# Six windowed attention layers: reciprocal lengths seeded by exp(-ln/2) on ScalarE, and masks as two products over separate row halves

## The chip, the core and the metric

One core of a Trainium2 chip. The metric is the device time of one execution in microseconds (us). Engines: TensorE (PE; its weight loads are shown apart as PEld), VectorE (DVE), ScalarE (ACT), GpSimd (POOL) and the DMA queue of SyncE (SP). Each runs its own instructions in order and waits for the others through semaphores.

## The reference, cut to what matters

`x` is 8 sequences of 512 rows of 128 numbers. It is normalized, sent through a causal attention with relative positions, and, beside that, through six layers of windowed attention and feed-forward. The change touches the windowed attention only:

```python
def l2norm(t):
    return t / jnp.maximum(jnp.linalg.norm(t, axis=-1, keepdims=True), 1e-12)
# 16 heads of 64, windows of 32 queries, 64 keys each (own window and the one before)
q = l2norm(q) * qs;  k = l2norm(k) * ksc
q = q * cos * scale + rotate_half(q) * sin * scale      # k likewise, with 1 / scale
mask = (it < jb) | (it > jb + w) | (jb == -1)
sim = jnp.einsum('bhwie,bhwje->bhwij', bq, bk2) * QK_SCALE
sim = jnp.where(mask, -jnp.finfo(sim.dtype).max, sim)
out = einsum(softmax(sim), bv2) @ Wo
for i in range(6):
    x = attn_layer(shift_tokens(x), ...) + x
    x = ffn_layer(shift_tokens(x), ...) + x
```

## The kernel before, in words

`relative_attention` does the first attention (to about 560 us). `windowed_layers` then runs six layers, five in a hardware loop and the last one behind it. In each layer the 32 tiles of 128 rows (8 sequences by 4) go through a pipeline of slots: in the slot of tile T the engines project tile T (age 0), turn and score tile T-1 (age 1) and finish the softmax, the mixing and the output of tile T-2 (age 2). The order within a slot is written out by hand for every engine in a function called `slot`, and what one engine needs of another it waits for by counted semaphores. The two slots at the end of a layer (CLOSING and LAST) have no new tile and take in the first steps of the feed-forward part, which `feed` goes on with. `opening` projects the first tile of the next layer inside `feed`, so the first slot of a layer is that of tile 1.

TensorE in a full slot, in order: projection of v, k, k, q (each three products of 512 columns, L1250 to L1252), turning the first half of the weights (transposes, L1264), projection of q, turning the other weights, mixing (64 small products, L1288), turning q, mixing, projection of v, turning k, the mixed values, k again, then the two mask products (L1404), scores of four head pairs (L1274), output (L1410), scores of the other four. A mask product writes one PSUM bank (2 or 3, 128 rows by 512 columns) as identity times mask with start=True; the scores of even heads are then added into bank 2, those of odd heads into bank 3, by products with 64 contracting rows and 32 outputs each, head parity being the row half.

The lengths of T: ScalarE squares q and k (L1562), VectorE sums the squares by head (`square_sum`, L1747), and `square_root` bounds the 128x32 sums below (L1755), seeds the reciprocal root by a shift and a subtraction on number bits (L115, L117), halves the sums (L118) and does one Newton step (L121, L123, L125). GpSimd, which has meanwhile added the two parts of the rotated k and q (L1176), takes the result, does two more steps (`rsqrt_refine`, L139 to L145, eight instructions) and scales q and k by it (L1181). TensorE turns q and k in the next slot once they are scaled. On odd tiles GpSimd also makes the low part of the next inputs (L1057), after ScalarE has made the high part (`split_half`). VectorE's next work after the lengths is the output's addition (L1826) and then the maxima of the scores (L1782), the differences (L1788), from which ScalarE makes the weights by Exp (`weigh`, L1587).

ScalarE's functions come in table sets. Gelu (L1664) and Exp are in different ones, so a layer loads two.

Of the kernel before, what the change touches and what calls it, by code (L numbers as in the profile page):

```python
# [27 lines left out]
P = 128  # L28
B, N, D = 8, 512, 128
TPS = N // P  # L30
H = 16
# [3 lines left out]
W = 32  # L35
# [18 lines left out]
C_NEAR = C_FART + P  # L54
# [6 lines left out]
def constants():  # L61
# [21 lines left out]
    first = (np.arange(P)[:, None] < W) & (k2 < W)  # L83
    c[:, C_MQ0:C_MQ0 + 2 * W] = np.where(first, MASKED, shut)
    far = np.where(np.arange(P)[None, :] >= np.arange(P)[:, None], MASKED, 0.0)
    c[:, C_FAR:C_FAR + P] = far
    c[:, C_FART:C_FART + P] = far.T
# [785 lines left out]
def windowed_layers(nc, Wqkv, qs, ks, Wout, ln_g, ln_b, W1, b1, W2, b2, state, total, rank, out):  # L873
# [8 lines left out]
    with ExitStack() as ctx:  # L882
# [24 lines left out]
        half_ss, rn_tmp = sb("half_ss", [P, 2 * H]), sb("rn_tmp", [P, 2 * H])  # L907
# [26 lines left out]
        id_bf, mask_bf, mean_w = rank["id_bf"], rank["mask_bf"], rank["mean_w"]  # L934
# [3 lines left out]
        FIRST_STEPS, MORE_STEPS = 1, 2  # L938
        RN_FIRST, RN_MORE = 1 + 3 + 3 * FIRST_STEPS, 4 * MORE_STEPS
# [25 lines left out]
        rn_chain, rn_more = sem("rn_chain"), sem("rn_more")  # L965
# [183 lines left out]
        def _(pool):  # L1149
# [18 lines left out]
            def rope_and_scale(lay, s, t):  # L1168
# [16 lines left out]
                pool.wait_ge(rn_chain, RN_FIRST * (T + 1))  # L1185
# [61 lines left out]
        def _(pe):  # L1247
# [45 lines left out]
            def slot(lay, s, t, ages):  # L1293
# [106 lines left out]
                if score:  # L1400
                    turn_k(1)
                    pe.wait_ge(on_made, at(T, 2, 2, 2))
                    for par in range(2):
                        pe.matmul(PS[:, 2 + par, :], id_bf[:], bc(mask_q[tile1], 1, PAIRS),  # L1404
                                  start=True, stop=False, skip_group_check=True)
                    score_half(0)
# [127 lines left out]
        def _(act):  # L1534
# [18 lines left out]

            def high_part(lay, i):
                act.wait_ge(raw_in[i], 16 * lay + 16)
                last_projected(act, lay)
                copy(w_hi[:, third(i)], w_raw[:, third(i)]).then_inc(hi_made, 1)
# [22 lines left out]
            def slot(lay, s, t, ages):  # L1580
# [67 lines left out]
                if 0 in ages:  # L1648
                    new = next_half(s, t)
# [17 lines left out]
            def feed(lay, follows):  # L1667
# [15 lines left out]
                if follows:  # L1683
                    split_half(lay + 1, 0, 1)
# [6 lines left out]
            copy(credit[:, 47:48], zeros[:, 0, 0:1]).then_inc(gel_made, 2)  # L1691
            high_part(0, THIRDS[0])
# [3 lines left out]
            for n in range(len(OPENING)):  # L1696
                opening(0, n)
            split_half(0, 0, 1)
# [6 lines left out]
        def _(dve):  # L1705
# [44 lines left out]
            def square_root(T):  # L1750
# [4 lines left out]
                dve.tensor_scalar(ss[:], ss[:], 1e-24, None, ALU.max).then_inc(rn_chain, 1)  # L1755
                dve.wait_ge(rn_chain, RN_FIRST * T + 1)
                rsqrt_steps(dve, rn_chain, RN_FIRST * T + 1, rn[:], ss[:], half_ss[:], rn_tmp[:], FIRST_STEPS)
# [12 lines left out]
            def lengths(T):  # L1770
                square_sum(T, 0, sqq_made)
                square_sum(T, 1, sqk_made)
                square_root(T)
# [177 lines left out]
```

## Time and profile before

| | us |
|---|---|
| median of 3 runs | 3954.44 (3954.09 to 3967.59) |
| the profiled execution | 3959.98 |
| its span, first to last instruction | 3958.2 |
| mean granted clock of TensorE | 0.982 of full speed |

Busy shares of the span by the profile's page: PE 94%, PEld 72%, DVE 83%, ACT 55%, POOL 66%. To read the rows: times are us from the span's start, "xN" counts instructions, and what stands in square brackets is the idle time of the engine just ahead of the row and who ended it. A matmul's start is recorded and its end is modelled, so overlapping products show in the distances of their starts, not in their busy time. "issue" is idle time for which the profile shows nothing to wait for.

### The profile page before, as it was taken

To read this page: it belongs to the slowest core of one execution; us is meant where nothing else is said; L and a number is where in the kernel's file an instruction comes from. 1 tells how busy PE (TensorE), PEld (TensorE's weight loads), DVE (VectorE), ACT (ScalarE), POOL (GpSimd) and SP (SyncE) were. 2 spreads that over 40 slices of the span, in tenths; PEclk is the share of its full clock that TensorE was granted. 3 is DMA by queue.
4 is the path that set the end of the run, shared out by engine and by line. 5 is a ranking of instruction groups with operands and counts; after the bars stand their busy time and mean duration, and the time that the engine had idled before them with its cause. 6 is when DMAs were issued, how large, how long until landed. Compare 5 with 4: busy or idle time off the path is not lost.

```text
span 3958.2 us, 165481 instructions
## 1 busy us (share of the span) xinstructions
PE 3716.9 (94%) x67712; PEld 2864.8 (72%) x67712; DVE 3286.9 (83%) x6981; ACT 2178.6 (55%) x3886; POOL 2598.7 (66%) x3029
## 2 busy tenths in 40 slices
PE   6999979999999999999999999999999999999998
PEld 3555547878767787677787677787677776777776
DVE  7666659999789899788998798997889897888886
ACT  3555545666546666456665465665466564565552
POOL 4555538887457777368787287874577773687770
PEclk8999989999999999999999999999999999999999
DMA  1000012222212222122222122222122221222220
GB/s 43 4 6 4 6 34 66 57 56 59 58 34 58 60 60 58 35 53 56 60 60 52 33 65 60 56 57 56 35 57 60 60 56 37 53 55 59 60 52 22
DMA packets 136325, 189.11 MB, mean 48 GB/s; under 512 B 38006, under 2 KB 58484, under 8 KB 135412
## 3 DMA queue, kind: packets, MB, share of 16 engines
q1 hardware_dynamic: 135540, 178.17, 17.6%
q8 instruction: 551, 9.03, 1.0%
q14 instruction: 234, 1.92, 0.2%
HBM read 22.61 MB, written 2.10 MB: 6 GB/s over the span
## 4 chain that ended last, share of the span: by engine, by line
POOL 39%; PE 22%; issue 20%; DVE 2%; POOLq 2%; ACT 0%; DMA 0%; SPq 0%; DVEq 0%; ACTq 0%
POOL t L1176 18%; POOL t L1181 8%; PE PS L1264 3%; PE PS L1250 3%; POOL xl L1057 3%; PE PS L1469 2%; PE PS L1252 2%; PE PS L1251 2%; POOL rn L145 2%; PE PS L1410 2%; POOL rn_tmp L141 2%; POOL rn_tmp L143 2%; POOL rn_tmp L139 2%; PE PS L1288 2%; PE PS L1274 1%
## 5 line engine op out<-in xcount | busy, mean ns | idle before, releaser
L1176 POOL TENSOR_TENSOR t<-t 128x1024 f32<-128x1024 f32 x384 | 908.3, 2373 | 263.3 <-DVE t L1742 263.3
L1535 ACT ACTIVATE va<-PS 128x512 f32<-128x512 f32 x384 | 230.1, 599 | 956.3 <-PE PS L1252 956.3
L1181 POOL TENSOR_TENSOR t<-t,rn 128x1024 f32<-128x1024 f32 x384 | 724.1, 1907 | 28.4 <-POOL rn L145 25.9
L1740 DVE TENSOR_TENSOR t<-PS,rope 128x512 f32<-128x512 f32 x768 | 521.7, 679 | 23.6 <-ACT sq L1562 18.1
L1250 PE MATMUL PS<-w_hi,xh 128*128 128x512 f32 x1152 | 514.8, 447 | 25.7 <-DVE xl L1057 10.1
L1562 ACT ACTIVATE sq<-PS 128x512 f32<-128x512 f32 x768 | 455.7, 594 | 38.3 <-PE PS L1252 22.3
L1252 PE MATMUL PS<-w_lo,xh 128*128 128x512 f32 x1152 | 460.8, 400 | 0.0
L1251 PE MATMUL PS<-w_hi,xl 128*128 128x512 f32 x1152 | 458.9, 398 | 0.0
L1264 PE MATMUL PS<-constants,t 128*128 128x128 f32 x3072 | 444.7, 278 | 9.5 <-POOL t L1181 7.6
L1747 DVE TENSOR_REDUCE ss<-sq 128x16 f32<-128x1024 f32 x384 | 448.0, 1207 | 0.0
L1264 PEld LDWEIGHTS PS<-constants,t 128*128 128x128 f32 x3072 | 352.8, 142 | 58.2 <-POOL t L1181 9.9
L1410 PE MATMUL PS<-oT,w_out 128*128 128x128 f32 x3072 | 393.3, 281 | 0.0
L1288 PE MATMUL PS<-vs,shared 64*32 64x65 f32 x18432 | 337.2, 225 | 45.3 <-issue 45.3
L1410 PEld LDWEIGHTS PS<-oT,w_out 128*128 128x128 f32 x3072 | 357.8, 191 | 17.7
L1274 PEld LDWEIGHTS PS<-kT,qT 64*32 64x32 f32 x24576 | 273.9, 105 | 127.3 <-issue 103.3
L1274 PE MATMUL PS<-kT,qT 64*32 64x64 f32 x24576 | 342.7, 225 | 15.0 <-POOL kT L1210 7.8
L1288 PE MATMUL PS<-va,shared 64*32 64x65 f32 x6144 | 338.9, 225 | 14.6 <-issue 14.6
L1288 PEld LDWEIGHTS PS<-vs,shared 64*32 64x32 f32 x18432 | 265.0, 105 | 111.0 <-issue 110.8
L1741 DVE TENSOR_TENSOR t<-PS,rope 128x256 f32<-128x256 f32 x768 | 316.3, 412 | 0.0
L1742 DVE TENSOR_TENSOR t<-PS,rope 128x256 f32<-128x256 f32 x768 | 315.8, 411 | 0.0
L1782 DVE TENSOR_REDUCE m<-PS 128x16 f32<-128x1024 f32 x192 | 234.9, 1224 | 87.4 <-PE PS L1274 85.2
L1250 PEld LDWEIGHTS PS<-w_hi,xh 128*128 128x128 f32 x1152 | 218.3, 190 | 95.7 <-issue 30.0
(172 smaller groups left out, 8112.8 us busy)
## 6 DMA issues: line engine op xcount, KB each, us to landing
vs<-va SPq DMA_DIRECT2D x768, 130.0 KB
vs<-va SPq DMA_DIRECT2D x768, 65.0 KB
t<-in_L_ffn_Wqkv SPq DMA_DIRECT2D x18, 512.0 KB, 4.4
w_out<-in_L_ffn_Wo SPq DMA_DIRECT2D x6, 512.0 KB, 3.9
a_normed<-in_L_attn_x SPq DMA_DIRECT2D x8, 256.0 KB, 6.4
a_xo<-in_L_attn_x SPq DMA_DIRECT2D x8, 256.0 KB, 2.9
out<-total SPq DMA_DIRECT2D x8, 256.0 KB, 3.5
w_raw<-in_L_ffn_W SPq DMA_DIRECT2D x6, 341.0 KB
```

What stands on the lines that cost most here:

```text
L1176: pool.tensor_tensor(mine[:, i, :], mine[:, i, :], t2[:, i, :], ALU.add).then_inc(done, 1)
L1181: pool.tensor_tensor(h, h, bc(rn[:, H * i:H * (i + 1)], 2, HB), ALU.mult).then_inc(done, 1)
L1250: pe.matmul(out, hi, w_hi, start=True, stop=False)
L1251: pe.matmul(out, lo, w_hi, start=False, stop=False)
L1252: return pe.matmul(out, hi, w_lo, start=False, stop=True)
L1264: last = pe.transpose(PS[:, bank, P * j:P * (j + 1)], source(j), ident)
L1274: last = pe.matmul(PS[W * w:W * (w + 1), 2 + par, 2 * W * pair:2 * W * (pair + 1)], qT[rows, pair, W * w:W * (w + 1)], kT[rows, t % 2, pai ...
L1288: last = pe.matmul(PS[W * w:W * (w + 1), (0, 2)[c] + par, HB1 * (pair % 4):HB1 * (pair % 4 + 1)], pT[rows, pair, W * w:W * (w + 1)], v, st ...
L1410: last = pe.matmul(PS[:, y_at, 0:P], w_out[:, pair, :], oT[:, pair, :], start=(pair == 0), stop=(pair == PAIRS - 1))
L1562: act.activation(sq[:, i, 512 * c:512 * (c + 1)], PS[:, bank, :], ACT.Square).then_inc(done, 1)
L1740: dve.tensor_tensor(o1, src, bc(rope[:, 2 * i, t, :], 1, 8), ALU.mult)
L1747: dve.tensor_reduce(ss[:, H * i:H * (i + 1)], sq[:, i, :].rearrange("p (h d) -> p h d", h=H), X, ALU.add).then_inc(ss_made, 1)
```

## The change

The bound and the halving become one VectorE instruction with two operations. The seed is made on ScalarE as exp(-ln(-2 * half)/2), two instructions of 128x32, in the same table set, which is loaded ahead of it (and of the layer's later Exp). VectorE's six further instructions go. GpSimd's two Newton steps stay. ScalarE's `seed(T)` stands behind the second k copy of the slot and ahead of `split_half`; in `feed` it stands behind the last piece of the opening.

The mask products contract over 64 rows each, rows 0 to 63 for bank 2 and rows 64 to 127 for bank 3, with a new 128x128 constant that selects for each query its row of the mask within a half. The constants grow by 128 columns. In the diff below, the pieces behind `seed` are those of ScalarE's `slot`, its `feed`, its start ahead of the first layer, and GpSimd's `rope_and_scale`.

```diff
+C_SEL = C_FART + P
-    first = (np.arange(P)[:, None] < W) & (k2 < W)
+    first = (np.arange(P)[:, None] % (2 * W) < W) & (k2 < W)
+    row, query = np.arange(P)[:, None] % (2 * W), np.arange(P)[None, :]
+    c[:, C_SEL:C_SEL + P] = np.where(query < W, query == row, query % W + W == row)
...
                     for par in range(2):
-                        pe.matmul(PS[:, 2 + par, :], id_bf[:], bc(mask_q[tile1], 1, PAIRS),
+                        rows = slice(HB * par, HB * (par + 1))
+                        pe.matmul(PS[:, 2 + par, :], sel_bf[rows, :], bc(mask_q[tile1][rows, :], 1, PAIRS),
                                   start=True, stop=False, skip_group_check=True)
...
-            def square_root(T):
+            def half_squares(T):
                 dve.wait_ge(ss_made, at(T, 0, 2, 2))
                 dve.wait_ge(kn_made, at(T, 1, 1, 1))
-                dve.tensor_scalar(ss[:], ss[:], 1e-24, None, ALU.max).then_inc(rn_chain, 1)
-                dve.wait_ge(rn_chain, RN_FIRST * T + 1)
-                rsqrt_steps(dve, rn_chain, RN_FIRST * T + 1, rn[:], ss[:], half_ss[:], rn_tmp[:], FIRST_STEPS)
+                dve.tensor_scalar(half_ss[:], ss[:], 1e-24, -0.5, ALU.max, ALU.mult).then_inc(half_made, 1)
...
+            def seed(T):
+                act.wait_ge(half_made, T + 1)
+                act.activation(ln_ss[:], half_ss[:], ACT.Ln, scale=-2.0).then_inc(ln_made, 1)
+                act.wait_ge(ln_made, T + 1)
+                act.activation(rn[:], ln_ss[:], ACT.Exp, scale=-0.5).then_inc(seed_made, 1)
...
                 if 0 in ages:
+                    seed(T)
                     new = next_half(s, t)
...
                 if follows:
+                    act.preload_act_table_set("natural_log_exp_and_others")
+                    seed(number(lay + 1, 0, 0))
                     split_half(lay + 1, 0, 1)
...
+            act.preload_act_table_set("natural_log_exp_and_others")
...
+            seed(0)
             split_half(0, 0, 1)
...
-                pool.wait_ge(rn_chain, RN_FIRST * (T + 1))
+                pool.wait_ge(seed_made, T + 1)
```

## Rows read from the trace of the kernel before

**Rows 1.** The page's engine line, and the stretch of 30 slots of layer three.
```profile
PE 3716.9 (94%) x67712; PEld 2864.8 (72%) x67712; DVE 3286.9 (83%) x6981; ACT 2178.6 (55%) x3886; POOL 2598.7 (66%) x3029
...
1716.20:2155.50 439.30, 423.79 (x9707) 346.44 (x9705) 399.89 (x870) 267.78 (x514) 348.33 (x422) 1.00 0.24 59
```

**Rows 2.** The chain that ended last, shares of the span by engine.
```profile
POOL 39%; PE 22%; issue 20%; DVE 2%; POOLq 2%; ACT 0%; DMA 0%; SPq 0%; DVEq 0%; ACTq 0%
```

**Rows 3.** Timeline of TensorE around one slot: start, duration, line, tiles, count.
```profile
1199.83 0.60 PE L1264 MATMUL PS<-constants,t 128*128 128x128 f32 x4
1200.27 0.59 PE L1404 MATMUL PS<-mask_bf,id_bf 128*128 128x512 bf16 x2
1200.79 0.86 PE L1274 MATMUL PS<-kT,qT 64*32 64x64 f32 x64
...
1204.35 0.50 PE L1250 MATMUL PS<-w_hi,xh 128*128 128x512 f32 x1
...
1218.83 0.49 PE L1250 MATMUL PS<-w_hi,xh 128*128 128x512 f32 x1
```

**Rows 4.** Waits of TensorE over the span: total, times, longest.
```profile
PE PS L1288 <- issue: 59.9, 76, 1.5
```

**Rows 5.** Timeline of TensorE in that slot: four transposes, then the small mixing products.
```profile
1208.62 0.60 PE L1264 MATMUL PS<-constants,shared 128*128 128x128 f32 x4
1209.15 0.24 PE L1288 MATMUL PS<-vs,shared 64*32 64x65 f32 x1
```

**Rows 6.** Groups by form over the span: the mask products (busy, mean ns, idle before).
```profile
L1404 PE MATMUL PS<-mask_bf,id_bf 128*128 128x512 bf16 x384 | 115.2, 382 | 0.0
```

**Rows 7.** Timelines around one slot's lengths, and ScalarE's 128x128 Exp by form.
```profile
1202.36 0.20 DVE L1755 TENSOR_SCALAR ss<-ss 128x32 f32<-128x32 f32 x1
1203.56 0.19 DVE L125 SCALAR_TENSOR_TENSOR rn<-rn_tmp,rn 128x32 f32<-128x32 f32 x1
1203.83 0.24 POOL L139 TENSOR_TENSOR rn_tmp<-rn 128x32 f32<-128x32 f32 x1 [1.31 <-DVE rn L125]
1201.21 0.85 ACT L1535 ACTIVATE xh<-state 64x256 fp32r<-64x256 f32 x2
1205.36 0.60 ACT L1535 ACTIVATE va<-PS 128x512 f32<-128x512 f32 x1 [3.29 <-PE PS L1252]
L695 ACT ACTIVATE a_p<-a_d 128x128 f32<-128x128 f32 x8 | 2.5, 312 | 0.0
```

**Rows 8.** Timelines of four engines in a layer's first slot: layer six, then layer one.
```profile
3400.68 0.50 PE L1250 MATMUL PS<-w_hi,xh 128*128 128x512 f32 x1
3398.66 2.29 DVE L115 TENSOR_SCALAR rn<-ss 128x32 int32<-128x32 int32 x1
3403.98 1.22 DVE L1782 TENSOR_REDUCE m<-PS 128x16 f32<-128x1024 f32 x1
3398.55 4.72 POOL L1176 TENSOR_TENSOR t<-t 128x1024 f32<-128x1024 f32 x2
3404.15 0.24 POOL L139 TENSOR_TENSOR rn_tmp<-rn 128x32 f32<-128x32 f32 x1 [0.88 <-DVE rn L125]
3406.77 3.77 POOL L1181 TENSOR_TENSOR t<-t,rn 128x1024 f32<-128x1024 f32 x2
3406.01 1.28 ACT L1587 ACT_TABLE_LOAD   x1 [3.02 <-DVE shared L1788]
3411.74 1.06 PE L1264 MATMUL PS<-constants,t 128*128 128x128 f32 x6
...
606.73 1.09 PE L1264 MATMUL PS<-constants,shared 128*128 128x128 f32 x4 [2.56 <-ACT shared L1587]
```

**Rows 9.** Timelines of GpSimd and VectorE in the closing slot of layer two.
```profile
1597.57 0.24 POOL L139 TENSOR_TENSOR rn_tmp<-rn 128x32 f32<-128x32 f32 x1 [1.31 <-DVE rn L125]
...
1604.35 2.04 POOL L1201 TENSOR_TENSOR t<-t 128x512 f32<-128x512 f32 x2
1607.53 0.17 DVE L1715 TENSOR_SCALAR f_var<-PS 128x8 f32<-128x8 f32 x1 [3.12 <-PE PS L1440]
```

More of the change, by code:

```diff
@@ L53 @@
 C_FART = C_FAR + P
-C_NEAR = C_FART + P
+C_SEL = C_FART + P
+C_NEAR = C_SEL + P
 C_PART = C_NEAR + H
@@ L906, in windowed_layers @@
         halves3 = sb("halves3", [P, 2 * H])
-        half_ss, rn_tmp = sb("half_ss", [P, 2 * H]), sb("rn_tmp", [P, 2 * H])
+        half_ss, rn_tmp, ln_ss = sb("half_ss", [P, 2 * H]), sb("rn_tmp", [P, 2 * H]), sb("ln_ss", [P, 2 * H])
         qT = sb("qT", [P, PAIRS, P])
@@ L933, in windowed_layers @@
         ident = rank["const"][:, C_ID:C_ID + P]
-        id_bf, mask_bf, mean_w = rank["id_bf"], rank["mask_bf"], rank["mean_w"]
+        mask_bf, mean_w = rank["mask_bf"], rank["mean_w"]
+        sel_bf = mask_bf[:, C_SEL - C_MQ:C_SEL - C_MQ + P]
         mask_q = {t: mask_bf[:, 2 * W * (t == 0):2 * W * (t == 0) + 2 * W] for t in range(TPS)}
         RN_OPS = RSQRT_OPS + 1
-        FIRST_STEPS, MORE_STEPS = 1, 2
-        RN_FIRST, RN_MORE = 1 + 3 + 3 * FIRST_STEPS, 4 * MORE_STEPS
+        MORE_STEPS = 2
+        RN_MORE = 4 * MORE_STEPS
         CREDIT = 4
@@ L964, in windowed_layers @@
         ss_made = sem("ss_made")
-        rn_chain, rn_more = sem("rn_chain"), sem("rn_more")
+        half_made, ln_made, seed_made, rn_more = sem("half_made"), sem("ln_made"), sem("seed_made"), sem("rn_more")
         addq_made, addk_made = sem("addq_made"), sem("addk_made")
@@ L1772, in lengths @@
                 square_sum(T, 1, sqk_made)
-                square_root(T)
+                half_squares(T)
             def slot(lay, s, t, ages):
```

## The prediction

> **What bounds the kernel now.** I read four views, from the coarse to the fine. The busy shares come first: in 30 slots of layer three, 439.3 us or 14.6 us a slot, TensorE is busy for 423.8, VectorE for 399.9, GpSimd for 348.3 and ScalarE for 267.8 [rows 1]. The chain that ended last puts 39% on GpSimd and 22% on TensorE [rows 2], so the second question is which of the two a slot waits for. The chain follows GpSimd from one add to the next, but the adds wait for VectorE, which waits for the scores, which are TensorE's. So I went to TensorE's timeline. One slot runs from 1204.35 to 1218.83, 14.48 us [rows 3], and its products start at distances that their columns set: four transposes take 0.44 (1199.83 to 1200.27), the masks 0.52 (to 1200.79). What remains idle in most slots is inside the small products, put down to "issue": 59.9 us at L1288 in 76 waits [rows 4], of which the change touches nothing. GpSimd, 1.3 us of idle time in its lengths included [rows 7], is a follower with some slack. So in a full slot only what TensorE itself does counts, and the lengths count only where TensorE does wait: in the first slot of a layer and in the first closing slot.
>
> **The change part by part. The seed.** Removed from VectorE is the stretch from the end of L1755 (1202.36 + 0.20) to the end of L125 (1203.56 + 0.19), 1.19 us; the one instruction left costs what L1755 costs, 0.20 [rows 7]. GpSimd started its steps at 1203.83, 1.27 behind L1755. In its place come two ScalarE instructions of 128x32. The trace has none of that size; a 128x128 one takes 0.31 [rows 7], which bounds each from above, and I take 0.25. With three hand-overs of some 0.08 each (L125's end at 1203.75 to 1203.83) that is 0.75, so GpSimd begins about 0.5 us earlier; the bounds are 0.4 (0.31 each and hand-overs of 0.09) and 0.8 (ScalarE at the 0.2 that small instructions of VectorE take, hand-overs hidden in part).
>
> In a full slot this is worth nothing. It is covered by TensorE's own 14.5 us; if that cover were gone, GpSimd would be the bound, and the 0.5 would count in full.
>
> What is queued behind the new wait on ScalarE: `split_half` (0.85) and then the next slot's copy of v, which frees bank 7 for the q product. The high part was made at 1201.21, now about 1203.3 to 1204.1, and the v copy starts at 1205.36 after 3.29 us of waiting for TensorE [rows 7]. So 1.2 us are left and this costs nothing. At the opening of the first layer and ahead of the last, where no loop turn lies between, the margin is smaller and up to 1 us may be lost once each; I take 1 in all. The low part on GpSimd comes two scalings later and is not late.
>
> **First slots.** Here the small VectorE instructions stand beside GpSimd's long add (4.72 us from 3398.55), and two of them are held until one of its halves ends: L115 took 2.29 instead of 0.2, and the next one as long [rows 8]. The maxima, ready to start at about 3400.8, when the scores have ended (TensorE's next product starts at 3400.68), start at 3403.98. The change takes these instructions away, so the maxima come 3.2 us earlier, and in the last layer the Exp table's load of 1.28, which stood behind the differences, has gone ahead too. TensorE would reach the turning of q 4.5 us earlier, at 3407.2. But GpSimd is late next: its steps began at 3404.15 and can begin no earlier than the add's end, 3403.27; the first of the two scalings, 1.9 of the 3.77 from 3406.77, then ends at 3407.8 instead of 3408.7. So q is turned at about 3407.9 instead of 3411.74: 3.8 us. The same working on the first layer, where TensorE waited 2.56 for the weights [rows 8], gives 2.3, and on the four between 0.6, 2.7, 0 and 0.6. Six first slots: 10 us. Should the remaining instruction be held once (up to 2.3), the maxima still start near the scores' end; the low bound is 5. The high bound is 14: behind layer one's wait the four transposes take 1.09 instead of 0.60 [rows 5, 8], as at half the clock, and shorter waits may save some of that.
>
> **Closing slots.** GpSimd's 1.31 wait for the seed [rows 9] is followed, without a gap, by its steps, the scaling and the squares of the feed-forward norm (from 1604.35); VectorE waits 3.12 us for the sums of these squares, and TensorE in turn for VectorE's root. Here the 0.5 counts: 6 x 0.5 = 3 us.
>
> The table loads stay two a layer, at 1.28 each [rows 8]. The one that moves into `feed` stands where ScalarE has to wait for VectorE's sums anyway, and the one added ahead of the first layer is followed by the wait for the rope's scales. Both cost nothing.
>
> The Trainium skill (ScalarE: Activation LUTs, What ACT_TABLE_LOAD costs) gives 1.28 us and 1.38 of drain, 2.66 in all. The trace agrees with the first figure [rows 8]; of the second no row here tells.
>
> **The masks.** Now two products of 512 columns start 0.21 apart (0.59 for both less the 0.38 of one [rows 3, 6]), and the scores start 0.31 behind the second, of which 0.21 are its columns and 0.10 the change to 64 rows. The same 0.09 to 0.10 stand between transposes and mixing: 0.53 for four transposes instead of 0.44 [rows 3, 5]. From the last transpose to the first score it is 0.11 + 0.21 + 0.31 = 0.63 us. After: the change to 64 rows comes ahead of the masks (0.11 + 0.09 = 0.20), the two start together if the halves work side by side (0.01), and the scores, which have other output columns, start 0.31 behind: 0.52, a gain of 0.11. The weights of 128 columns can't be loaded ahead over such a change; no row shows their cost in this form, and I take 0.03 to 0.05 for it from the 0.10 that a mask's load leaves under its predecessor now. So 0.07 a slot. In the six first slots TensorE waits behind the mask anyway, so 186 x 0.07 = 13 us. Part of it is lost where TensorE next stands in an "issue" wait, which depends on when its instructions were fetched and not on when it arrives; a quarter gives 10 us. Bounds: -0.15 a slot (side by side fails, the load shows), -28 us; and +0.21 (the second product free, the first change no dearer than the one behind it, which goes), +39 us.
>
> The Trainium skill (TensorE: Matmul & The Clock Gate, Measured speedup vs the span model) has four products over 32 rows each at 512 columns run 3.07 times as fast as in a row, which speaks for the overlap. It also says (TensorEngine Tiling (Array Packing), Key Properties) that changing the tiling mode drains TensorE; that is the 0.10 of rows 3 and 5, and it speaks against this edit, since a second such change may be bought for one product.
>
> The constants grow by a sixteenth or so and load once, under 0.5 us.
>
> **The sum.** 10 + 3 + 10 - 1 = 22 us. From the profiled execution's 3960.0 that makes 3938; this execution lies 5.5 above the median of the runs shown, 3954.4, so the forecast in runs is 3932.
>
> **The rivals.** (A) The forecast, 3932: 0.37. (B) The halves don't work side by side: the masks take 0.21 + 0.09 more than hoped, so 0.09 to 0.15 a slot is lost, 17 to 28 us, against 12 gained elsewhere: 3960 to 3970, slower than before. For it: no row shows two products over 64 rows that fill all 128 outputs, and the small products are spaced by their weight loads, so their overlap by row halves isn't proven. It decides where two masks take more than 0.32 from start to the scores plus 0.10. 0.18. (C) The masks gain nothing, because two changes and a bare weight load eat the 0.2, or because the "issue" waits do: 12 us, 3942. Nothing in the rows speaks against it, 0.25. (D) The change between the two 64-row forms is free and the gain per slot is 0.2: 186 x 0.2 = 37, plus 12: 3905. The change from 128 to 32 outputs alone would have to cost nothing. 0.15. (E) It doesn't do what it says: the table sets alternate in every slot, each load of 1.28 standing ahead of the weights, for which TensorE is waiting or about to. 186 x 1.28 is 238 us; with half of it covered it is 119, so 4060 or above. The set named has both functions. 0.02. The rest, 0.03, is a start of the first layer or an alignment of TensorE's fetches that comes out worse.
>
> The gain of the seed in first and closing slots, 12 us, is in A to D alike. The range takes in A and C whole, B up to 3964 and D down to 3906: 3906 to 3964.
>
> Chances, where 0.5% (20 us, about what a measurement of this kernel can tell from no change) divides: faster, under 3934.7, is D, most of A and the top of C, 0.46; slower, over 3974, is E, the end of B and half of the rest, 0.08; within 0.5%, 0.46. The likeliest case, A, has a range of its own, 3925 to 3938.
>
> **What would show it.** Right, if GpSimd's L139 starts about 0.75 behind the new VectorE instruction; if the maxima of the first slots follow the scores' end at once; if the waits of ScalarE's va copy stay above a microsecond; if the second mask starts within 0.05 of the first, with the scores 0.3 behind it. Wrong, if a row of the va copy is released by anything but TensorE, if a table load stands in a full slot, or if the two masks start 0.2 apart. The prediction as a whole falls if full slots change in length by more than 0.2 us either way, since 186 of them outweigh all that the seed does.

## The result, and the profile after

| | before | after |
|---|---|---|
| median of 7 runs each | 3965.22 (3954.09 to 3969.12) | 3937.53 (3927.25 to 3938.96) |
| ratio | | 0.9933, interval 0.9916 to 0.9950 |
| profiled execution, its span | 3959.98, 3958.2 | 3928.65, 3926.6 |

The change saves 27.7 us. The forecast of 3932 was the level of the kernel before, 3954.4, less a gain of 22. The three runs before on which it stood were low: the seven give 3965, and in four later comparisons the median of the same kernel lay between 3962 and 3972. So the level was 11 us too low and the gain 6 us too small, and the two errors partly cancel in the forecast. A single execution says little below 10 us: the runs of either kernel spread over 12 to 15.

The page of the kernel after: its engine line, then the stretch of the same 30 slots of layer three, from first mask to first mask (columns as in [rows 1]).

```profile
PE 3690.6 (94%) x67712; PEld 2844.7 (72%) x67712; DVE 3058.0 (78%) x5829; ACT 2270.7 (58%) x4270; POOL 2597.4 (66%) x3029
...
1710.26:2149.40 439.14, 424.51 (x9852) 347.21 (x9852) 364.05 (x693) 283.68 (x576) 351.24 (x428) 1.00 0.24 61
```

Thirty slots with VectorE 36 us less busy, and with GpSimd's steps started some 0.67 us earlier (below), take the same 439 us as before [rows 1]. So the lengths don't set this stretch. It doesn't show the 0.11 a slot that the masks save either, 3 us in thirty slots; the experiments below say where that goes. The chain that ended last now follows TensorE, where before it followed GpSimd for 39% [rows 2]:

```profile
PE 76%; issue 4%; DVE 2%; POOL 2%; ACT 0%; DMA 0%; POOLq 0%; SPq 0%; DVEq 0%; ACTq 0%
```

That line looks like a change of regime, and it isn't one: full slots are within 0.1 us of what they were. That two engines are nearly as long as each other here, so that a shift of 0.7 us decides which of them the chain is led along, is my reading and not tested.

TensorE's timeline at the masks of one slot, which answers [rows 3]:

```profile
1210.13 0.60 PE L1270 MATMUL PS<-constants,t 128*128 128x128 f32 x4
1210.66 0.39 PE L1411 MATMUL PS<-mask_bf 64*128 64x512 bf16 x2
1210.98 0.86 PE L1280 MATMUL PS<-kT,qT 64*32 64x64 f32 x64
```

Two products of 512 columns now take 0.39 together; before they took 0.59. From the transposes' row to the scores' it is 0.85 instead of 0.96 (1199.83 to 1200.79). By the starts of single products, medians of 192 slots that hardly vary: last transpose to first mask 0.109 before and 0.205 after, mask to mask 0.215 and 0.003, mask to score 0.309 and 0.316. In sum 0.633 and 0.524.

The waits of TensorE at the mixing products, as in [rows 4]: 4.5 us more than before.

```profile
PE PS L1294 <- issue: 64.4, 87, 1.4
```

The seed, in the closing slot of layer two (VectorE, then GpSimd): GpSimd begins 0.80 behind the start of VectorE's instruction, where it was 1.47 (1202.36 to 1203.83, [rows 7]); from that instruction's end it is 0.60 instead of 1.27. Its wait is 0.64 instead of 1.31. VectorE's wait for the sums of the squares is 2.76 instead of 3.12 [rows 9]. By form, over the span, the two new instructions take 229 ns each.

```profile
1590.18 0.20 DVE L1775 TENSOR_SCALAR half_ss<-ss 128x32 f32<-128x32 f32 x1
1590.98 0.24 POOL L144 TENSOR_TENSOR rn_tmp<-rn 128x32 f32<-128x32 f32 x1 [0.64 <-ACT rn L1567]
...
1601.15 0.17 DVE L1735 TENSOR_SCALAR f_var<-PS 128x8 f32<-128x8 f32 x1 [2.76 <-PE PS L1447]
...
L1565 ACT ACTIVATE ln_ss<-half_ss 128x32 f32<-128x32 f32 x192 | 44.0, 229 | 239.9 <-DVE half_ss L1775 239.9
L1567 ACT ACTIVATE rn<-ln_ss 128x32 f32<-128x32 f32 x192 | 44.0, 229 | 6.1
```

The first slot of layer six, which answers [rows 8] (VectorE, GpSimd, ScalarE, TensorE):

```profile
3374.73 1.96 DVE L1775 TENSOR_SCALAR half_ss<-ss 128x32 f32<-128x32 f32 x1
3376.61 1.21 DVE L1800 TENSOR_REDUCE m<-PS 128x16 f32<-128x1024 f32 x1
3374.29 4.73 POOL L1182 TENSOR_TENSOR t<-t 128x1024 f32<-128x1024 f32 x2
3378.97 0.24 POOL L144 TENSOR_TENSOR rn_tmp<-rn 128x32 f32<-128x32 f32 x1
3376.72 0.23 ACT L1565 ACTIVATE ln_ss<-half_ss 128x32 f32<-128x32 f32 x1 [2.84 <-DVE half_ss L1775]
3383.56 1.09 PE L1270 MATMUL PS<-constants,t 128*128 128x128 f32 x8 [1.58 <-POOL t L1187]
```

One VectorE instruction is still held (1.96 instead of 0.20) until the first of GpSimd's two additions ends; before there were two in a row. The maxima stand at VectorE's first free moment, GpSimd goes on with no wait, and TensorE, as forecast, now waits 1.58 for GpSimd's scaled q. It does so in all twelve first slots of two traces of the change: q is turned 0.05 to 0.06 behind the end of GpSimd's first scaling.

Where the 31.6 us between the two profiled spans lie (a slot is measured from the start of its first mask product to the next slot's):

| | before | after | gain |
|---|---|---|---|
| ahead of the first mask | 598.4 | 597.4 | 1.0 |
| 6 first slots | 105.0 | 88.0 | 17.0 |
| 174 full slots | 2533.3 | 2521.8 | 11.5 |
| 6 closing slots | 122.6 | 121.9 | 0.7 |
| 5 times ending and feed | 503.9 | 501.4 | 2.5 |
| behind the last mask | 95.0 | 96.2 | -1.2 |

### The profile page after: what moved, and what is told of

It reads as the page before. It is cut to its first block, busy times and chain, and to the rows that moved or that the text cites. A ratio compares the mean times of both kernels' runs of the same rounds, so it can differ in the third digit from the quotient of the medians.

```text
span 3926.6 us, 163773 instructions
## 1 busy us (share of the span) xinstructions
PE 3690.6 (94%) x67712; PEld 2844.7 (72%) x67712; DVE 3058.0 (78%) x5829; ACT 2270.7 (58%) x4270; POOL 2597.4 (66%) x3029
## 4 chain that ended last, share of the span: by engine, by line
PE 76%; issue 4%; DVE 2%; POOL 2%; ACT 0%; DMA 0%; POOLq 0%; SPq 0%; DVEq 0%; ACTq 0%
PE PS L1270 18%; PE PS L1417 10%; PE PS L1256 10%; PE PS L1294 8%; PE PS L1280 8%; PE PS L1258 8%; PE PS L1257 8%; PE PS L1476 2%; PE PS L1411 2%; PE PS L1454 1%; PE PS L1447 1%; POOL t L1182 1%; PE PS L1442 1%; POOL t L1187 0%; DVE m L1800 0%
## 5 line engine op out<-in xcount | busy, mean ns | idle before, releaser
L1182 POOL TENSOR_TENSOR t<-t 128x1024 f32<-128x1024 f32 x384 | 908.0, 2370 | 363.9 <-DVE t L1762 362.6
L1542 ACT ACTIVATE va<-PS 128x512 f32<-128x512 f32 x384 | 229.8, 599 | 614.4 <-PE PS L1258 611.6
L1270 PE MATMUL PS<-constants,t 128*128 128x128 f32 x3072 | 443.8, 277 | 19.8 <-POOL t L1187 12.8
L1256 PEld LDWEIGHTS PS<-w_hi,xh 128*128 128x128 f32 x1152 | 217.4, 189 | 92.5 <-issue 24.7
```

The lines of the kernel that those rows point to most:

```text
L1182: pool.tensor_tensor(mine[:, i, :], mine[:, i, :], t2[:, i, :], ALU.add).then_inc(done, 1)
L1256: pe.matmul(out, hi, w_hi, start=True, stop=False)
L1270: last = pe.transpose(PS[:, bank, P * j:P * (j + 1)], source(j), ident)
```

## The experiments

All ratios are against the kernel before in the same comparison. "Second halves" are the mean lengths of the second half of the mixing and of the scores in full slots, where the waits ended by issue show: undisturbed, each takes 0.79. The profile counts 64 instructions in such a half where the code has 32 products. The last three columns are from single traces; two traces of one kernel differ by 0.015 and 0.025 in the mean full slot.

| kernel | ratio (interval) | mean full slot | 6 first slots | second halves |
|---|---|---|---|---|
| before, two traces | 1 | 14.559, 14.544 | 105.0, 107.6 | 1.21, 0.91; 1.21, 0.89 |
| the change, two traces | 0.9933 (0.9916 to 0.9950), 0.9920 (0.9898 to 0.9942) | 14.493, 14.518 | 88.0, 86.0 | 1.23, 0.92; 1.25, 0.93 |
| seed only | 0.9934 (0.9910 to 0.9958) | 14.487 | 90.7 | 1.17, 0.89 |
| masks only | 0.9981 (0.9963 to 0.9998) | 14.455 | 107.2 | 1.19, 0.92 |
| masks on one row half | 0.9977 (0.9960 to 0.9995) | 14.574 | 87.5 | 1.12, 0.84 |
| one step on GpSimd | 0.9908 (0.9881 to 0.9935) | 14.471 | 80.9 | 1.23, 0.91 |
| before, all steps on GpSimd | 1.0033 (1.0018 to 1.0048) | 14.625 | 109.0 | 1.13, 0.90 |
| scores together | 1.0158 (1.0138 to 1.0178) | 14.965 | 88.0 | see there |
| the same, one step | 1.0133 (1.0111 to 1.0156) | 15.033 | | |
| values between mixings | 0.9906 (0.9888 to 0.9925) | 14.441 | 89.4 | 0.86, 0.83 |
| the same, one step | 0.9884 (0.9864 to 0.9904) | 14.467 | 79.0 | 0.87, 0.84 |
| halving on GpSimd | 0.9941 (0.9920 to 0.9961) | 14.538 | 94.6 | |

**The two parts apart.** The change with the masks as before:

```diff
-                        rows = slice(HB * par, HB * (par + 1))
-                        pe.matmul(PS[:, 2 + par, :], sel_bf[rows, :], bc(mask_q[tile1][rows, :], 1, PAIRS),
+                        pe.matmul(PS[:, 2 + par, :], id_bf[:], bc(mask_q[tile1], 1, PAIRS),
```

> The lengths' part of the change alone, with the masks as they were. My theory: it pays only where TensorE waits, in the six first slots (17 us in the profile of the changed kernel, 105.0 to 88.0) and little elsewhere, so the ratio to the kernel before is 0.9950 to 0.9965 (14 to 20 us). Full slots keep their length of 14.56 us on average within 0.03. Rival, that the lengths' chain through GpSimd, which the chain of waits of before put ahead of TensorE, sets the full slots too: these get shorter by 0.06 us or more, and this kernel is as fast as the whole change, 0.993.

Measured: 3938.22, ratio 0.9934, as fast as the whole change. And the kernel before with the masks of the change (the same lines the other way round, and the constants with them):

> The masks' part alone, with the lengths as they were. My theory: from the last transpose to the first score it takes 0.52 instead of 0.63 us, and of these 0.11 a slot some 0.06 arrive at the slot's end, 186 x 0.06 = 11 us, so a ratio of 0.997 (0.9955 to 0.9985), and the two parts add up to the whole. Rival, that the masks' gain is given back in full in the waits for instructions: ratio 0.9990 to 1.001, and the full slots stay at 14.56.

Measured: 3955.80, ratio 0.9981. The savings alone are 0.0066 and 0.0019, 0.0085 in sum; together they measured 0.0067 and 0.0080. So they add within the intervals, and the seed has about three quarters of it. The size I gave the seed is refuted, and both numbers of the rival came true (0.993, and full slots shorter by 0.065). Its mechanism, GpSimd's chain in full slots, is what the two experiments on GpSimd's steps speak against. The trace of the seed alone shows 90.7 us of first slots against 105.0 and 107.6.

In full slots the single traces don't add up: 0.065 with the seed alone, 0.097 with the masks alone (14.455), and 0.046 with both. The profiled execution of the masks alone was 9 us below the median of its runs, which is 0.05 a slot. So one trace doesn't tell how 0.05 of a full slot is shared out; the medians are what the shares above rest on.

**Side by side, or only 64 rows?** Both products on rows 0 to 63:

```diff
-                        rows = slice(HB * par, HB * (par + 1))
+                        rows = slice(0, HB)
```

> The whole change, but both mask products contract over rows 0 to 63, which hold the same masks, so they can't run side by side and the result is the same. My theory: the second mask starts 0.21 behind the first again, the first slot score 0.73 behind the last transpose instead of 0.52, and a full slot is longer than in the changed kernel by 0.13 to 0.21 us, 25 to 40 us in all: 3962 to 3977 against 3937, ratio to the kernel before 0.999 to 1.003. Rival, that the overlap doesn't matter because TensorE has slack at this place: within 5 us of the changed kernel.

Measured: 3956.03, ratio 0.9977, 18 us behind the change where I had 25 to 40, and full slots 0.06 to 0.08 longer where I had 0.13 to 0.21. TensorE's timeline in that kernel:

```profile
1210.14 0.60 PE L1270 MATMUL PS<-constants,t 128*128 128x128 f32 x4
1210.68 0.60 PE L1411 MATMUL PS<-mask_bf 64*128 64x512 bf16 x2
1211.21 0.97 PE L1280 MATMUL PS<-kT,qT 64*32 64x64 f32 x64
...
PE PS L1294 <- issue: 49.0, 67, 1.2
```

Mask to mask is 0.226 and transpose to mask 0.205, as in the change. So the 0.003 comes from the separate row halves, and the price of going to 64 rows, 0.096, is paid in both. The waits row shows what becomes of such time: masks and first scores take 0.29 us a slot more than in the change (0.21 and 0.08), and mixing waits 15 us less for issue; the two second halves are 0.11 and 0.08 shorter. Of 0.29, 0.06 to 0.08 arrives at the slot's length.

**One step less on GpSimd.** `MORE_STEPS = 1` in the change, so that GpSimd does four operations of 0.33 instead of eight:

> The whole change with one Newton step on GpSimd instead of two, four instructions less a tile, 1.3 us of GpSimd's chain. My theory: full slots don't get shorter, since GpSimd has slack there; the first slots do, where TensorE waits about 1.6 us for the scaled q (2.25 to 2.44 at the mixing products instead of 0.79), by 1.3 each, and the closing slots by up to 1 each: 8 to 12 us under the changed kernel, ratio to the kernel before 0.990 to 0.9915. Rival, that GpSimd is still a part of the full slots' length: 0.2 us or more a slot, 35 us and more, ratio 0.984 or less.

Measured: 3926.02, ratio 0.9908. The first slots fall from 88.0 to 80.9: 7 us, or six times 1.2, nearly the 1.3 of the step. It is GpSimd's chain that first slots wait for after the change. With the step gone, q is turned behind the scaling at once in two of the six, and 1.2 to 1.5 later in the other four. Full slots keep their length within 0.05. GpSimd's wait for VectorE ahead of the additions takes up the rest (the page's row, which reads 363.9 in the change):

```profile
L1182 POOL TENSOR_TENSOR t<-t 128x1024 f32<-128x1024 f32 x384 | 909.2, 2369 | 595.1 <-DVE t L1762 595.1
```

**One step more on GpSimd.** The kernel before, with VectorE's step moved there (`FIRST_STEPS, MORE_STEPS = 0, 3`):

> The kernel before with its one refining step on VectorE moved to GpSimd (0 steps there, 3 on GpSimd), masks and seed bits as before. VectorE loses three operations of 0.19 us, GpSimd gains four of 0.33 us, 1.3 us a slot, against 263.3 us / 192 = 1.37 us a slot in which GpSimd waited for VectorE. My theory (full slots are not set by the chain of the lengths, so it may move by a microsecond either way): full slots within 0.1 us of 14.56, the six first slots 0 to 8 us longer in sum, ratio 0.998 to 1.004. Rival (GpSimd is at its edge in full slots, and the part of the seed's gain that full slots show comes from an earlier start of GpSimd): full slots longer by 0.3 to 1.3 us, ratio 1.013 to 1.06.

Measured: 3984.87, ratio 1.0033. Full slots are 0.07 to 0.08 longer, 13 us in sum; first slots 1 to 4 us longer, closing slots 132.2 instead of 122.6 and 124.0. Each lies where the theory had it except the closing slots, which I had not priced: there GpSimd's steps are followed by the squares of the norm without a gap, and the six lost 1.2 to 2.4 each, 1.6 in the mean. The products that spread the root begin 0.6 later in four of them and 1.5 in two (VectorE's own chain is shorter by its three operations); the rest is TensorE's clock, which stands at half for 45 us in the six slots instead of 24 and 30. The edit adds one wait besides, VectorE for the end of its own chain. Full slots have room for a GpSimd 1.3 us busier, but not quite for nothing.

**Scores in one piece.** The second half of the scores directly behind the first, ahead of the output; VectorE's addition of the output behind the next maxima:

```diff
                     score_half(0)
+                    score_half(1).then_inc(s_mm, 1)
                 if mix:
                     pe.wait_ge(oT_made, at(T, 2, 2, 2))
...
                     last.then_inc(y_mm, 1)
-                if score:
-                    score_half(1).then_inc(s_mm, 1)
```

> The change, and the second half of the scores directly behind the first, ahead of the output products, so that TensorE goes from 64-row to 128-row products and back once a slot and not twice; VectorE adds the output of a slot to the state behind the maxima of the next. Theory: each passage costs what the first mask product showed, 0.095 us, so two fewer are 0.19 us a slot, 35 us in 186 slots, a quarter of it lost to waits for instructions: ratio 0.985 to 0.989 against the kernel before, and 0.992 to 0.996 of the change. Rival: 128 small products in a row want instructions faster than they come, and the gain goes into waits ended by issue, or the maxima are later and GpSimd with them: ratio 0.992 to 0.998.

Measured: 4034.73, ratio 1.0158. Slower by 62 us, and both my cases had it faster. Timeline of TensorE in one slot, with ScalarE's second copy of the turned k, and two rows of TensorE's waits:

```profile
1827.05 0.39 PE L1411 MATMUL PS<-mask_bf 64*128 64x512 bf16 x2
1827.37 1.57 PE L1280 MATMUL PS<-kT,qT 64*32 64x64 f32 x106
1827.39 0.63 ACT L1541 ACTIVATE kT<-PS 128x512 f32<-128x512 f32 x1
1828.24 0.53 PEld L1280 LDWEIGHTS PS<-kT,qT 64*32 64x32 f32 x43 [0.18 <-issue]
1830.28 0.42 PE L1280 MATMUL PS<-kT,qT 64*32 64x64 f32 x22 [1.34 <-issue]
...
PE PS L1280 <- issue: 94.4, 63, 2.2
PE PS L1294 <- issue: 26.5, 40, 2.1
```

Two things happen here. After 106 score products TensorE stands still for 1.34 us with nothing to wait for. Stops of over 0.5 us come 62 times in the 174 full slots, behind 78 to 123 of the 128. The scores of a slot take 2.39 us in the mean instead of 1.71, the output 2.08 where it is 1.81 undisturbed, and the second mixing half 0.95 instead of 1.23. The rival named these waits, and was far too small on them.

The other is the step that failed in the theory: not the price of a passage, but what the output had covered. In the least disturbed slots scores and output take 3.51 us (1.71 and 1.81) against 3.56 in the change (0.79, 1.98, 0.79), a gain of 0.04 and not 0.19. But within the 1.71 there is a gap of 0.29 between the starts of the 64th and the 65th product (153 of 174 slots; neighbours start 0.017 apart there). In 167 of the 174 slots the 65th starts 0.255 behind the end of ScalarE's second copy of the turned k, while the gap itself varies from 0.14 to 0.51. In the slot above the copy ends at 1828.02 and the weights are loaded at 1828.24. The profile puts this wait down to issue. In the change the output products stand between and cover it. With neighbours 0.017 apart instead of the gap, the two passages fewer would have given some 0.3, an estimate from these distances.

> The scores together, and one refining step on GpSimd where the change has two. Theory: the gain of one step (3937.5 to 3926.0 us, 11 us) adds to that of the scores together, as one lies in first slots and the other in full ones: ratio 0.982 to 0.986. Rival: with the scores together the step off GpSimd is worth nothing or all: within 0.001 of the kernel with the scores together alone.

Measured: 4024.90, ratio 1.0133. The step is worth 10 us here as well; the scores together are what the theory had wrong.

**The change once more.**

> The change itself once more, for a second trace. If the gain of the profiled executions in full slots is a property of the code, their mean is within 0.03 us of 14.493; if it is scatter between executions (the runs of each kernel spread over 10 us, 0.05 us a slot), it may be up to 14.56. Ratio 0.9915 to 0.995; the second mask product starts 0.003 us behind the first and the six first slots sum to 86 to 91 us either way.

Measured: 3939.09, ratio 0.9920; full slots 14.518, first slots 86.0.

**Long products between short ones.** If runs of short products wait for instructions, long ones in between should help. In the change, the second half of the values goes between the two mixing halves:

```diff
+                if project_new:
+                    pe.wait_ge(rq_made, at(T, 0, 2, 1))
+                    project(2, 1, 6, t, v_mm)
                 if mix:
                     mix_half(1)
-                if project_new:
-                    pe.wait_ge(rq_made, at(T, 0, 2, 1))
-                    project(2, 1, 6, t, v_mm)
```

> The change, with the twelve long products of the second half of the values (0.80 us) between the two mixing halves instead of behind them, so that no two runs of 128 short products lie within 1 us of each other. In the change the second mixing half takes 0.79 us in 103 of 174 full slots and up to 2.4 us in the other 71, 0.44 us a slot in the mean, ended by the arrival of instructions. Theory (instructions come at a limited rate, and short products use up what was fetched ahead): 0.80 us of long products in between let them catch up, mixing falls by 0.2 to 0.4 us a slot, ratio 0.975 to 0.985 against the kernel before. Rival one (the fetch stops at places of the program, whatever runs there): the stall is the same in sum and moves to other lines, ratio 0.991 to 0.995. Rival two (the bank of the second values half is not free yet, and the values wait for VectorE): TensorE waits up to 0.8 us there, ratio 1.00 to 1.02.

Measured: 3929.67, ratio 0.9906. TensorE's waits at the mixing products:

```profile
PE PS L1294 <- issue: 9.5, 28, 2.1
```

64.4 us has become 9.5: the second mixing half fell by 0.37 us a slot, the second score half by 0.09. That rules out the first rival, a stall that only moves, although the ratio is nearly the one it gave.

The traces also tell what ends these waits. The page has a queue of instructions, here that of the change:

```profile
q8 instruction: 551, 9.03, 1.0%
```

These are 551 packets of 16 KB, one every 5.4 us in the median. All 72 waits of the change over 0.3 us at the mixing products end 1.1 to 1.7 us behind the end of one of these packets, as do the 64 and 63 in the two traces of before and 58 of the 62 over 1 us at the scores of the kernel with the scores together; of the mixing products that didn't wait, 9% start at such a distance. So TensorE waits for its next instructions. That the queue is TensorE's is an inference from the counts: its 135,424 recorded instructions are 246 a packet, and 128 short products, each with its weight load, are 256, so a row of short products uses up about a packet in under 3 us.

The ratio doesn't hold, since a new wait took most of the gain. The 16 transposes behind the second mixing half need 2.19 us instead of 1.84. The gap opens ahead of those that turn the second half of the mixed values, whose row in one slot is 1.32 long (second line below), while VectorE's normalising of these values ends at 1806.17 + 0.69 (first line):

```profile
1806.17 0.69 DVE L1830 TENSOR_TENSOR on<-PS,rden 128x512 f32<-128x512 f32 x1
1806.31 1.32 PE L1270 MATMUL PS<-constants,on 128*128 128x128 f32 x8
```

In the change the 0.80 of values products covered that. Of 0.46 gained a slot, 0.34 is given back there and 0.08 by the values themselves (0.90 instead of 0.82); in the medians 8 us are left. The second rival named a wait of another place, the bank's; there is none there. The step of the theory that failed is that the products moved away covered nothing.

> The same with one refining step on GpSimd instead of two. Theory: the 11 us of one step (3937.5 to 3926.0) lie in the first slots and come on top: 0.0025 to 0.0035 below the kernel with two steps. Rival: within 0.001 of it.

Measured: 3918.44, ratio 0.9884, 0.0022 below, just short of what I gave; the first slots are 10 us shorter (79.0 against 89.4). With the values between and one step it is the fastest kernel here, 19 us under the change.

**The kernel before once more.**

> The kernel before once more, for a second trace. If the 0.07 us a slot by which the full slots of the change were shorter than the kernel before is a property of the code, the mean of this trace is 14.55 to 14.60 us; if it is scatter, it may be anywhere from 14.49 to 14.62. The six first slots sum to 102 to 108 us either way.

Measured: full slots 14.544, just below the band I gave, first slots 107.6. With two traces each, the full slots are 14.552 before and 14.506 after: 0.046 a slot, 8 us, where the profiled pair alone had 11.5.

**The last VectorE instruction.** The halving on GpSimd, the logarithm on the sums themselves:

```diff
-                dve.tensor_scalar(half_ss[:], ss[:], 1e-24, -0.5, ALU.max, ALU.mult).then_inc(half_made, 1)
...
+                pool.wait_ge(ss_made, at(T, 0, 2, 2))
+                pool.tensor_tensor(half_ss[:], ss[:], minus_half[:], ALU.mult).then_inc(half_made, 1)
+                pool.wait_ge(half_made, T + 1)
                 pool.wait_ge(seed_made, T + 1)
...
-                act.activation(ln_ss[:], half_ss[:], ACT.Ln, scale=-2.0).then_inc(ln_made, 1)
+                act.activation(ln_ss[:], ss[:], ACT.Ln).then_inc(ln_made, 1)
```

> The change with its one VectorE operation on the lengths (maximum and half of the squares) taken away: ScalarE takes the logarithm of the sums themselves, and GpSimd makes the half squares, in the time in which it waits for the seed anyway. Left out: the clamp of the sums at 1e-24. In the change that operation takes 0.20 us in 185 slots and 0.6 to 2.35 us in the others, five of them in first slots, beside GpSimd's addition. Theory (what is held there delays the maxima, but TensorE's first mixing group waits for GpSimd's scaled q anyway): maxima up to 2 us earlier, first slots shorter by 0 to 6 us in sum, ratio 0.992 to 0.994. Rival (the held operation is what first slots still lose): first slots shorter by 6 to 12 us, ratio 0.990 to 0.992. A second rival (the logarithm now runs beside the addition and is held like VectorE was): ScalarE's operation over 1 us and first slots no shorter.

Measured: 3938.91, ratio 0.9941. The first slots are 94.6, longer and not shorter. The maxima start 0.04 to 0.20 behind the scores' end in all six (0.04 to 0.44 in the change), but the halving lies on GpSimd's chain, directly behind the additions:

```profile
603.24 0.27 POOL L1193 TENSOR_TENSOR half_ss<-ss,minus_half 128x32 f32<-128x32 f32 x1
603.59 0.24 POOL L144 TENSOR_TENSOR rn_tmp<-rn 128x32 f32<-128x32 f32 x1
```

Six times 0.35 is 2 us of the 6.6. Most of the rest is TensorE's clock. In layers three, five and six the granted clock is 0.89 to 0.90 of full speed over the first slot and 1.00 in the other three; there TensorE takes 5.8 us from the turning of q to the next first mask, and 4.46 in the others and in nearly all of the change. That is 4.1 us. The clock fell behind the wait for the scaled q; the other three had waits about as long and kept it, so the wait's length alone doesn't decide it. A product of 512 columns in it takes 0.63 to 0.79 instead of 0.40 to 0.50:

```profile
1725.22 0.79 PE L1260 MATMUL PS<-w_hi,xh 128*128 128x512 f32 x1
1725.81 0.63 PE L1261 MATMUL PS<-w_hi,xl 128*128 128x512 f32 x1
```

Both rivals fall: the held instruction cost nothing any more, and ScalarE's, beside the same addition, isn't held.

## Why the prediction was right, and which of its steps were not

**The bound.** Full slots are TensorE's, first slots are not: right. VectorE lost 36 us in 30 slots and their length stayed; with 1.3 us less on GpSimd full slots stayed within 0.05, and with 1.3 us more they were 0.07 to 0.08 longer.

**The seed's chain.** Forecast from the end of VectorE's instruction to GpSimd's start 0.75, so 0.5 earlier (0.4 to 0.8); measured 0.60 and 0.67. ScalarE's instructions take 0.23, not 0.25, and the three hand-overs 0.03, 0.03 and 0.08, not 0.08 each (1590.38 to 1590.98).

**Full slots by the seed: 0.** Not settled. With the seed alone the trace has 14.487, 0.065 below the mean of the two of before, 11 us in sum, and the medians ask for something like it (26 us against 15.6 in first slots). One trace can't tell. 0.05 of the 0.065 lies in the two second halves, in waits ended by issue. That VectorE's six fewer instructions a slot make room for TensorE's is a guess that no run tests.

**What waits behind the seed on ScalarE.** Right: ahead of the 384 v copies ScalarE is idle for 614.4 us, 1.6 each, of which TensorE ends 611.6. The 1 us set aside wasn't needed: the first mask of layer one comes 1.0 earlier. The table loads are 13 in all, 1283 ns each, none in a full slot. The one moved into `feed` was free ahead of layer six: ScalarE waited 1.57 us for VectorE's sums behind it (to 3364.84).

**First slots: 10 us (5 to 14).** The waits were right in sum and the size was wrong: 17.0 in the profiled pair, 19 by two traces each, 15.6 with the seed alone, all above the high bound. The term that was mis-sized is TensorE's clock, which stands in the prediction only as a chance in the high bound ("as at half the clock"). The windows of the six first slots in sum, and that of layer three, before and then after (columns as in [rows 1], the granted clock third from the end):

```profile
sum 104.96, PE 80.23 PEld 63.36 DVE 96.08 ACT 51.06 POOL 83.39; mean PE 13.37 PEld 10.56 DVE 16.01 ACT 8.51 POOL 13.90
1716.18:1734.94 18.76, 13.62 (x310) 10.82 (x308) 17.12 (x29) 8.52 (x17) 13.92 (x16) 0.91 0.31 73
...
sum 87.95, PE 73.27 PEld 58.40 DVE 76.57 ACT 52.45 POOL 80.96; mean PE 12.21 PEld 9.73 DVE 12.76 ACT 8.74 POOL 13.49
1710.26:1724.40 14.14, 12.42 (x309) 9.81 (x308) 12.22 (x22) 8.59 (x18) 13.43 (x16) 0.96 0.41 98
```

TensorE is idle for 24.7 us before and for 14.7 after: 10.0, the number forecast. The other 7.0 are busy time, 80.2 against 73.3, for the same products. The masks are 1.2 of it. The 5.8 left go with the granted clock, 0.86 to 0.96 in the six windows before and 0.96 to 1.00 after: half clock fills 19.7 us of the six slots before and 2.3 after. That it's the shorter waits that keep the clock up is argued from this, and no run sets it apart. The second pair of traces says the same (idle 12.9, busy 8.7; clock 0.83 to 0.98 and 0.96 to 1.00).

That the idle time came to 10.0 is partly luck. By layer the forecast was 2.3, 0.6, 2.7, 0, 0.6 and 3.8; the whole gains are 2.8, 1.4, 4.6, 1.2, 4.1 and 2.9, the idle time's part 1.2, 0.8, 3.4, 0.2, 2.9 and 1.6. Before, the maxima started 2.66, 2.80, 3.46, 0.04, 2.45 and 3.24 us behind the scores' end, now 0.04 to 0.44: six times 2.14 is 12.8. The 0.04 of layer four, on which its forecast of 0 stands, doesn't come again: the second trace of before has 2.81 there and 2.81 to 3.77 in all six. The scores' end itself comes 5.7 earlier in sum, and behind the maxima 1.5 is given back, as TensorE now waits for the scaled q. In layer three of before the scores wait 1.65 for GpSimd's copy of k; when this copy starts against the first mask varies from slot to slot, -0.2 to 2.6 us before and -0.5 to 1.3 after, and what moves it stays open. Feed and first slots together gave 21 us (608.9 and 615.0 against 589.4 and 591.5), so it isn't only a shift across the mark.

**Closing slots: 3 us.** About half of it: 122.6 and 124.0 before, 121.9 and 121.8 after. The forecast gain does reach TensorE. The products that spread the root start 95.8 and 95.9 us behind the first masks before, the six added up, and 93.5 and 92.1 after: 3.0 less by the means. Half of that is lost behind them, where TensorE's clock stands at half for longer: for 23.8 and 30.0 us of the six slots before, 30.0 and 34.0 after. What it costs, in layers one and two of the change:

```profile
1032.07:1050.39 18.32, 15.56 (x344) 12.56 (x344) 11.43 (x29) 6.39 (x14) 10.22 (x14) 1.00 0.18 47
1588.21:1609.06 20.85, 17.95 (x344) 14.87 (x344) 12.29 (x30) 6.65 (x14) 10.22 (x14) 0.84 0.16 41
```

In both the root's products start 15.46 behind the mask, and with the clock at half the slot is 2.5 us longer. The prediction put this term at nothing.

**The masks: 0.07 a slot, 10 us.** Right in sum by two errors that cancel. The distances gave 0.110, not 0.07: the weight load that I priced at 0.03 to 0.05 shows nowhere. And more than the quarter I took went to issue: the second halves grew by 0.05 to 0.06 (1.21 to 1.24, 0.90 to 0.92 in the means of two traces), and 0.046 a slot is left, 8 us, which the seed's part in full slots, if it has one, would share. The kernel with the masks alone measured 7.5 us.

**The rivals.** B falls with the 0.003 us between the masks, D with the 0.096 for the first passage. The Trainium skill's rule that changing the tiling mode drains TensorE (TensorEngine Tiling (Array Packing), Key Properties) speaks of that 0.096, and the trace agrees that such a passage costs time; by it the edit might have lost what it gained, and it didn't. C's second reason, the waits ended by issue, is half true: of 0.109 a slot some 0.05 goes into the two second halves.

**The level.** The forecast of the time came out near by two errors that partly cancel: a level 11 us too low and a gain 6 us too small. By two traces each the parts of the gain are 19.3 us in first slots, 8.0 in full slots, 1.5 in closing slots and 4.5 outside of them, where the forecast had 10, 10, 3 and -1. That the sum came within 6 us is no proof of its terms.

## What to carry to other kernels

An engine's saved work counts where another engine waits for it; find those places by the distance from the releasing work's end to the next start (2.44 us in the mean of six slots here), not by busy shares. Price the clock with the wait: a wait that gets shorter can give back more in the products behind it (5.8 us beside 10.0 here), and one that doesn't can take half of a gain (the closing slots). Where short products run in long rows, TensorE runs out of instructions, and a shorter step ahead of them is partly paid back as waits that the profile puts down to issue; spread them between long products. Before moving work, look for what it covered where it stood: the output covered ScalarE's copy of k, and the products of the values covered VectorE's normalising. In both moves that took most of what they gained. Take the level of the kernel before from more than three runs when the gain sought is 0.5%.

## What was not expected of the hardware

Two products on separate row halves, 64 rows by 128 outputs and 512 columns each, start 3 ns apart and by the profile's ends are both done after 390 ns; on the same half they start 226 ns apart, and both on all 128 rows 215.

Short products run undisturbed at 0.79 us for 64, but not for ever: after 106 in a row TensorE stood for 1.34 us, and 12 long products in between took 64.4 us of such waits down to 9.5. They end 1.1 to 1.7 us behind a packet of the queue of instructions.

VectorE's one instruction on 128x32 numbers, the halving, takes 0.18 us when no addition of GpSimd is under way. In the other 187 of 192 slots one is, and the halving ends 0.04 to 0.05 us behind the addition's end in every one of them: it takes 0.20 in most, since the addition is about to end, and 1.13 to 2.35 in the six first slots. ScalarE's of the same size takes 0.23 in either case, and VectorE's sum of the squares (1.21) isn't held by the same additions. By the Trainium skill (SBUF — State Buffer, SBUF: two separate sides) GpSimd and some of VectorE's instructions share one pair of ports as an exclusive lock, and ScalarE never waits for anyone; the rows agree.

In the closing slots TensorE's granted clock falls from 1.00 to half, 1.2 GHz, over the stretch in which it waits for VectorE's root, with 1.94 us busy of 3.40, and it is still at 0.54 in the 3.6 us of full work behind (here in layer three, columns as in [rows 1]):

```profile
2144.97:2158.60 13.63, 12.50 (x319) 9.87 (x318) 7.63 (x16) 5.08 (x12) 10.22 (x14) 1.00 0.24 62
2158.60:2162.00 3.40, 1.94 (x9) 1.58 (x8) 2.31 (x11) 1.05 (x2) 0.00 (x0) 0.50 0.02 5
2162.00:2165.62 3.62, 3.62 (x19) 3.45 (x18) 2.35 (x4) 0.53 (x1) 0.00 (x0) 0.54 0.00 0
```

The products that spread the root take 2.9 to 3.4 us there from the first start to the last in all six layers of both traces of before, and in eleven of the twelve of the change. In the twelfth, layer one, the clock stays at 1.00 and they take 1.78. The change doesn't cure this; it makes it somewhat longer (above).
